# Attention over 128 graphs: a step's chunks start at the fourth slot of the next step, and turned tokens alternate with units of v

## The chip, the core and the metric

One core of a Trainium2 chip. The metric is device microseconds of one execution. TensorE (PE) multiplies and transposes, VectorE (DVE), ScalarE (ACT) and GpSimd (POOL) do the rest, and SyncE (SP) issues nearly all DMAs.

## The reference

128 graphs of 128 nodes with 384 features; 12 heads of 32. For each graph:

```python
h = maximum(layernorm(x), 0)
q, k, v = h @ Wq + bq, h @ Wk + bk, h @ Wv + bv          # split into 12 heads
scores = q @ k.T / sqrt(32) + beta * adj                  # per head, 128 x 128
scores = where(adj > 0, scores, -9e15)
out = softmax(scores) @ v
x = x + out
```

## The kernel before

**Tiling.** A step `s` takes 4 graphs, 512 tokens; there are 32 steps (0 to 31) and a step 32 that only drains. Everything that is multiplied is split into a high and a low part, so that each matrix product is three products (high by high, low by high, high by low). Double buffers are chosen by `par`, the parity of the step.

**Units.** The projection of a step has 13 units (`UNITS`): q0 to q2, k0 to k2 (128 output columns for all 512 tokens, nine matmuls of 512 columns), v0 to v3 (one graph each, nine matmuls of 384 columns) and three "turn" units, which transpose the next step's normalised tokens `hn` for 128 features (four transposes each). A unit fills one of three PSUM banks: `BANK[par][o] = (o + par) % 3`, so unit `o` needs the bank of unit `o - 3`. `bank_free` (L378) makes PE wait until that unit has been taken out: for q and k by the low part on DVE (`low_part`, L598, L604), for a turn by `turn_low` on DVE (L591, L594), for v by ACT's copy (L525).

**Slots.** A step is 12 slots `u`. The matmuls of the units are dealt to the slots by their columns (`PIECES`), and a slot also carries one chunk of attention of the step before: one graph and four heads. In PE's order a slot `u` is: the scores of chunk `u` (L436), the turned probabilities of chunk `u-1` (L444), the slot's pieces of projection (L424) and turns (L404), and the values of chunk `u-2` (L459 to L461). PE takes them strictly in this order. The pieces of the last slots are, before and after the change:

```
slot     before                               after
7        k2 m6-8, v0 m0-4                     the same
8        v0 m5-8, v1 m0-5                     v0 m5-8, turn0, v1 m0-2
9        v1 m6-8, turn0, v2 m0-3              v1 m3-8, turn1, v2 m0
10       v2 m4-8, turn1, turn2                v2 m1-8, turn2
11       v3 m0-8                              the same
```

**DVE's order in a slot** (L653 to L675): `bias_scores` of chunk `u` (mask added, row maximum; L624), where a graph's three chunks are done `invert_sums` (L640), `p_low` of chunk `u-1` (L630), `scale_out` (L645), then the masks (slots 4 and 7; L583, L588), `moments` of the next tokens in slots 0 to 3, and the low parts of units that ended in slot `u-1`. So the low part of k2, which ends in slot 7, is the last thing that DVE does in slot 8. Turns that ended in slot `u-1` follow in slot `u` in the same place.

**ACT's order in a slot**: `p_high` of chunk `u-1` (L535), four exponentials of chunk `u` (L510), the high parts of units that ended in this slot (L517, L525, L530).

**The spread.** q and k come out of the projection stacked by head on partitions. `spread` (L232) copies them, 12 DMAs for q and 12 for k, from `qT`/`kT` to `q_st`/`k_st`, where each head's three parts (high, low, high) lie on 96 partitions. It can start when the low part of q2 or k2 is done, and the first scores of the next step wait for all of it (L431 to L433). All these DMAs, the loads of `xs` and `adjs` and the stores are issued by SP in a written order (L250 to L273), each after its own wait, so that a later one can't pass an earlier one.

**GpSimd** adds the bias of v to x (`add_bias`, L308), normalises the next tokens (`rstd_of`, `normalise`), splits v into high and low (`split_v`, L313) and adds x to the output (`add_x`, L322), in an order written in its `step` (L328 to L355).

The loops: steps 0, 1, 30, 31 and 32 are written out, steps 2 to 29 run in a hardware loop of pairs (L198 to L207).

Of the kernel before, what the change touches and what calls it, by code (L numbers as in the profile page):

```python
# [21 lines left out]
def graph_attention_kernel(nc, x, adj, wq, bq, wk, bk, wv, bv, beta, out):  # L22
# [7 lines left out]
    TOK = G * N  # L30
    SLOTS = G * CH
    SCALE = float(HD) ** -0.5
    VW = HD + 1
# [6 lines left out]
    UNITS = ([("q", c) for c in range(CH)] + [("k", c) for c in range(CH)]  # L40
             + [("v", 0), ("v", 1), ("turn", 0), ("v", 2), ("turn", 1), ("turn", 2), ("v", 3)])
    NB = len(UNITS)
# [36 lines left out]
    with ExitStack() as ctx:  # L79
# [142 lines left out]
        def _(sp):  # L222
# [21 lines left out]
            def store(s, j):  # L244

                wait(sp, added, G * s + j + 1)
                sp.nop(nofuse=True)
                sp.dma_start(out_v[s, j], on[:, j % 2, :]).then_inc(stored[j % 2], 16)

            def step(s, par, looped=False):  # L250
                proj, attend = has(s, looped, 0, STEPS - 1), has(s, looped, 1, STEPS)
                if has(s, looped, 2, STEPS):
                    store(s - 2, G - 1)
                if has(s, looped, 0, STEPS - 3):
                    sp.wait_ge(xb_done, G * (s + 1))
                    sp.wait_ge(normed, G * (s + 1))
                    sp.nop(nofuse=True)
                    sp.dma_start(xs[:, par], x_v[s + 2]).then_inc(x_in[par], 16)
                if proj:
                    spread(s, par, "q")  # L260
                if attend:
                    store(s - 1, 0)
                if has(s, looped, 0, STEPS - 2):
                    sp.wait_ge(mask_done, s + 1)
                    sp.nop(nofuse=True)
                    sp.dma_start(adjs[:], adj_v[s + 1]).then_inc(adj_in, 16)
                if proj:
                    spread(s, par, "k")
                if attend:
                    store(s - 1, 1)  # L270
                    store(s - 1, 2)
                if s is STEPS:
                    store(s - 1, 3)  # L273

# [5 lines left out]
        def _(pool):  # L280
# [47 lines left out]
            def step(s, par, looped=False):  # L328
                proj, attend = has(s, looped, 0, STEPS - 1), has(s, looped, 1, STEPS)
                if proj:  # L330
# [23 lines left out]
                if s is STEPS:  # L354
                    add_x(s - 1, 1 - par, 3)  # L355
# [21 lines left out]
        def _(pe):  # L377
# [49 lines left out]

            def scores(s, par, u):

                j, c, n = u // CH, u % CH, SLOTS * (s - 1) + u  # L430
                if u == 0:  # L431
                    pe.wait_ge(q_in, 16 * 3 * HPC * s)
                    pe.wait_ge(k_in, 16 * 3 * HPC * s)  # L433
                wait(pe, biased_done, HPC * (n - 1))
                for i in range(HPC):
                    mm = pe.matmul(ps_s[u % 2][:, i * N:(i + 1) * N], q_st[0:STACK, 1 - par, i, c, j * N:(j + 1) * N],  # L436
                                   k_st[0:STACK, 1 - par, i, c, j * N:(j + 1) * N], start=True, stop=True)
                mm.then_inc(scores_done, 1)
# [7 lines left out]

            def values_of(g, vp, v, n, odd):

# [5 lines left out]
                for i in range(HPC):  # L454
                    h = c * HPC + i
                    o = ps_o[j % 2][:, h * VW:(h + 1) * VW]
                    high, low = pT[:, odd, 0, i, :], pT[:, odd, 1, i, :]
                    first, second = v1[:, vp, j, h, :], v2[:, vp, j, h, :]
                    pe.matmul(o, high, first, start=True, stop=False)  # L459
                    pe.matmul(o, low, first, start=False, stop=False)  # L460
                    mm = pe.matmul(o[:, 0:HD], high, second, start=False, stop=True)  # L461
                mm.then_inc(pv_done, 1)

            def step(s, par, looped=False):
                proj, attend = has(s, looped, 0, STEPS - 1), has(s, looped, 1, STEPS)
                ahead = has(s, looped, 0, STEPS - 2)
                drain = 2 if not looped and s == STEPS else 0
# [33 lines left out]
        def _(act):  # L501
            act.dma_start(xs[:, 0], x_v[0]).then_inc(x_in[0], 16)

            def exps(s, u):

                n, odd = SLOTS * (s - 1) + u, u % 2
                wait(act, turned, n - 1)
# [30 lines left out]
            def step(s, par, looped=False):  # L538
                proj, attend = has(s, looped, 0, STEPS - 1), has(s, looped, 1, STEPS)
                ahead = has(s, looped, 0, STEPS - 2)  # L540
                drain = 1 if not looped and s == STEPS else 0
                for u in range(SLOTS + drain):
                    n = SLOTS * (s - 1) + u
                    if attend and (looped or n >= 1):
                        p_high(n - 1, (u - 1) % 2)
                    if attend and u < SLOTS:
                        exps(s, u)
                    if proj:
# [18 lines left out]
        def _(dve):  # L567
# [46 lines left out]

            def bias_scores(s, par, u):

                n, odd = SLOTS * (s - 1) + u, u % 2
                dve.wait_ge(scores_done, n + 1)
                wait(dve, exp_done, HPC * (n - 1))
                if u == 0:  # L620
                    dve.wait_ge(mask_done, s)
                dve.nop(nofuse=True)
                for i in range(HPC):
                    dve.tensor_tensor_reduce(out=biased[:, odd, i, :], in0=ps_s[odd][:, i * N:(i + 1) * N],  # L624
                                             in1=mask[:, 1 - par, u // CH, :], scale=-1.0, scalar=3.0e38, op0=ALU.add,
                                             op1=ALU.min, accum_out=neg_max[:, odd, i:i + 1]).then_inc(biased_done, 1)
# [22 lines left out]
            def step(s, par, looped=False):  # L649
                proj, attend = has(s, looped, 0, STEPS - 1), has(s, looped, 1, STEPS)  # L650
                ahead = has(s, looped, 0, STEPS - 2)
                drain = 3 if not looped and s == STEPS else 0
                for u in range(SLOTS + drain):  # L653
                    n = SLOTS * (s - 1) + u
                    ended, late, j = attend and u % CH == 2 and (looped or n > CH), u < CH, (u // CH - 1) % G
                    if attend and u < SLOTS:
                        bias_scores(s, par, u)
                    if ended:
                        invert_sums(s - 1 - late, j)
                    if attend and (looped or n >= 1) and u - 1 < SLOTS:  # L660
                        p_low(n - 1, (u - 1) % 2)
                    if ended:
                        scale_out(s - 1 - late, j)
                    if proj and u == 4:
# [94 lines left out]
```

## Time and profile before

| | |
|---|---|
| median of 3 runs | 1191.81 us (1189.29 to 1191.97) |
| profiled execution | 1193.08 us, span 1191.3 us |
| granted clock of PE, mean | 0.969 |
| busy | PE 1068.0 us (90%), DVE 957.0 (80%), ACT 894.7 (75%), POOL 570.9 (48%) |
| DMA | 138.14 MB, mean 116 GB/s |

The span is from the first to the last instruction; the execution's own time is a little longer. A busy PE is not a PE at its peak, since the ends of its matmuls are modelled. The granted clock is a share of 2.4 GHz. What a step costs is best read from the times at which each slot's scores start (L436, four matmuls): from one to the next is one slot.

### The profile page before, as it was taken

The page shows a single profiled execution, that of the slowest core. Times are in us where ns is not written, and L with a number is a line of the kernel's source. Part 1 is how long each engine was busy: PE and PEld are TensorE (multiplying, and loading weights), DVE is VectorE, ACT ScalarE, POOL GpSimd, SP SyncE. Part 2 cuts the span into 40 slices and gives each one's busy share as a digit, 9 for nine tenths or more (in the row PEclk, how much of TensorE's full clock was granted, in tenths as well). Part 3 has the DMA queues.
Part 4 walks back from the last instruction along what each step waited for, and adds up shares of the span by engine and source line. Part 5 has one row for each costly group of instructions (what it writes and reads, how often), then busy time and mean ns, then how long its engine had stood idle before and what let it go on. Part 6 is the DMA issues. An engine that isn't in the chain of part 4 may idle for free.

```text
span 1191.3 us, 38643 instructions
## 1 busy us (share of the span) xinstructions
PE 1068.0 (90%) x10959; PEld 904.1 (76%) x10959; DVE 957.0 (80%) x4343; ACT 894.7 (75%) x2343; POOL 570.9 (48%) x756
## 2 busy tenths in 40 slices
PE   2799889999999999999999999999999999999875
PEld 1677777877787887778788777778877787888764
DVE  5478778888888888888888888878888888888764
ACT  2377768877787887777788787778877777887764
POOL 3735535445544545454454455454545445454421
PEclk9899999999999999999999999999999999999985
DMA  4434345444444544434554444454444345443330
GB/s 141 112 94 114 110 110 141 122 116 118 115 107 134 142 123 116 119 109 109 136 141 118 114 113 115 115 137 129 118 118 115 105 127 143 129 117 93 80 96 28
DMA packets 91030, 138.14 MB, mean 116 GB/s; under 512 B 15600, under 2 KB 66288, under 8 KB 90864
## 3 DMA queue, kind: packets, MB, share of 16 engines
q1 hardware_dynamic: 90336, 135.85, 42.4%
q14 instruction: 149, 1.22, 0.3%
q10 hardware_dynamic: 528, 0.79, 0.2%
q8 instruction: 17, 0.28, 0.1%
HBM read 35.91 MB, written 25.17 MB: 51 GB/s over the span
## 4 chain that ended last, share of the span: by engine, by line
PE 57%; SPq 14%; DVE 12%; issue 11%; DMA 5%; ACT 1%; POOL 1%; DVEq 1%; POOLq 0%; ACTq 0%
PE ps_p L424 35%; SPq L241 13%; PE ps_t L444 9%; PE ps_s L436 6%; DMA k_st<-kT 4%; DVE biased L624 4%; DVE kT L604 3%; PE ps_o L459 2%; PE ps_o L460 2%; PE ps_o L461 2%; DVE on L645 1%; DVE hT L594 1%; DMA beta_col<-in_L_gnn_beta 1%; PE ps_p L404 1%; ACT probs L510 1%
## 5 line engine op out<-in xcount | busy, mean ns | idle before, releaser
L624 DVE CUSTOM_DVE_ANT_0 biased<-ps_s,mask 128x128 f32<-128x128 f32 x1536 | 351.7, 284 | 181.0 <-PE ps_s L436 166.0
L510 ACT ACTIVATE probs<-biased,neg_max 128x128 f32<-128x128 f32 x1536 | 487.0, 391 | 7.4 <-DVE neg_max L624 7.0
L424 PE MATMUL ps_p<-hT,w 128*128 128x512 f32 x1728 | 475.2, 415 | 3.7 <-DVE w L733 3.7
L535 ACT ACTIVATE pT<-ps_t 128x512 f16<-128x512 f32 x384 | 229.3, 597 | 244.0 <-PE ps_t L444 242.9
L424 PEld LDWEIGHTS ps_p<-hT,w 128*128 128x128 f32 x1728 | 314.1, 193 | 61.5 <-issue 3.9
L630 DVE TENSOR_TENSOR pT<-ps_t,pT 128x512 f16<-128x512 f32 x384 | 256.9, 669 | 17.7 <-ACT pT L535 17.5
L444 PE MATMUL ps_t<-ident,probs 128*128 128x128 f32 x1536 | 241.6, 281 | 16.0 <-ACT probs L510 15.7
L326 POOL TENSOR_TENSOR on<-on,xb 128x384 f32<-128x384 f32 x128 | 128.5, 1004 | 264.4 <-DVE on L645 262.1
L424 PE MATMUL ps_p<-w,hT 128*128 128x384 f32 x1152 | 243.9, 348 | 0.0
L436 PE MATMUL ps_s<-k_st,q_st 96*128 96x128 f16 x1536 | 150.9, 221 | 55.6 <-DMA k_st<-kT 49.4
L424 PEld LDWEIGHTS ps_p<-w,hT 128*128 128x128 f32 x1152 | 193.5, 189 | 2.7
L318 POOL CAST v<-v_f 128x384 f16<-128x384 f32 x128 | 64.7, 505 | 267.4 <-ACT v_f L525 250.0
L459 PEld LDWEIGHTS ps_o<-v,pT 128*128 128x128 f16 x1536 | 123.8, 97 | 81.5 <-issue 53.9
L444 PEld LDWEIGHTS ps_t<-ident,probs 128*128 128x128 f32 x1536 | 166.2, 144 | 21.0 <-ACT probs L510 20.8
L459 PE MATMUL ps_o<-v,pT 128*128 128x33 f16 x1536 | 160.9, 181 | 1.1 <-DVE pT L630 1.1
L460 PE MATMUL ps_o<-v,pT 128*128 128x33 f16 x1536 | 155.7, 178 | 0.0
L461 PE MATMUL ps_o<-v,pT 128*128 128x32 f16 x1536 | 155.7, 177 | 0.0
L436 PEld LDWEIGHTS ps_s<-k_st,q_st 96*128 96x128 f16 x1536 | 90.6, 97 | 59.7 <-issue 59.7
L460 PEld LDWEIGHTS ps_o<-v,pT 128*128 128x128 f16 x1536 | 126.1, 97 | 1.1
L311 POOL TENSOR_TENSOR xb<-xs,bv_row 128x384 f32<-128x384 f32 x128 | 126.5, 1011 | 0.0
L624 DVE DVE_READ_ACCUMULATOR2_ANT neg_max<- 128x1 f32 x1536 | 126.5, 82 | 0.0
L461 PEld LDWEIGHTS ps_o<-v,pT 128*128 128x128 f16 x1536 | 124.2, 96 | 0.0
(59 smaller groups left out, 1073.0 us busy)
## 6 DMA issues: line engine op xcount, KB each, us to landing
q_st<-qT SPq DMA_DIRECT2D x384, 96.0 KB, 2.2
k_st<-kT SPq DMA_DIRECT2D x384, 96.0 KB, 2.1
out<-on SPq DMA_DIRECT2D x128, 192.0 KB, 1.9
xs<-in_x SPq DMA_DIRECT2D x31, 768.0 KB, 4.6
adjs<-in_adj SPq DMA_DIRECT2D x32, 256.0 KB, 2.9
xs<-in_x ACTq DMA_DIRECT2D x1, 768.0 KB, 6.9
k_st<-in_L_gnn_Wq SPq DMA_DIRECT2D x1, 576.0 KB, 5.3
k_st<-in_L_gnn_Wk SPq DMA_DIRECT2D x1, 576.0 KB, 7.4
```

Source lines behind the costliest of these rows:

```text
L241: sp.dma_start(dst[HD * b:HD * (b + 1), par, i], src[HD * i:HD * (i + 1), part]).then_inc(landed, 16)
L326: pool.tensor_tensor(on[:, j % 2, :], on[:, j % 2, :], xb[:, par, j, :], ALU.add).then_inc(added, 1)
L424: mm = pe.matmul(dst, stationary, moving, start=m == 0, stop=m == MMS - 1)
L436: mm = pe.matmul(ps_s[u % 2][:, i * N:(i + 1) * N], q_st[0:STACK, 1 - par, i, c, j * N:(j + 1) * N], k_st[0:STACK, 1 - par, i, c, j * N:(j ...
L444: mm = pe.transpose(ps_t[:, i * N:(i + 1) * N], probs[:, odd, i, :], ident[:])
L459: pe.matmul(o, high, first, start=True, stop=False)
L460: pe.matmul(o, low, first, start=False, stop=False)
L461: mm = pe.matmul(o[:, 0:HD], high, second, start=False, stop=True)
L510: act.activation(probs[:, odd, i, :], biased[:, odd, i, :], ACT.Exp, bias=neg_max[:, odd, i:i + 1], scale=-1.0).then_inc(exp_done, 1)
L535: act.activation(pT[:, odd, 0], ps_t[:].rearrange("p (h q) -> p h q", q=N), ACT.Copy).then_inc(p_high_done, 1)
L624: dve.tensor_tensor_reduce(out=biased[:, odd, i, :], in0=ps_s[odd][:, i * N:(i + 1) * N], in1=mask[:, 1 - par, u // CH, :], scale=-1.0, sc ...
L630: dve.tensor_tensor(pT[:, odd, 1], ps_t[:].rearrange("p (h q) -> p h q", q=N), pT[:, odd, 0], ALU.subtract).then_inc(p_low_done, 1)
```

## The change

Three things (the diff shows, in this order, the constants, `chunk`, SP, GpSimd and PE). A constant `LAG = CH = 3` moves the attention of a step's 12 chunks by three slots: chunk `v` of step `s-1` is scored in slot `v+3` of step `s`, so that the last three are scored in slots 0 to 2 of step `s+1`. In steps 1 to 31 all twelve slots still carry projection; slots 0 to 2 of step 1 have no chunk, and step 32 drains 15 chunks instead of 12. The function `chunk` tells for a slot and a distance behind it which chunk is due, with its step and parity. Second, the units are reordered so that turns alternate with v. Third, SP's and GpSimd's orders are rewritten to fit. Each graph's output is finished three slots later too: graph 0 in slot 8, graph 1 in slot 11, graphs 2 and 3 in slots 2 and 5 of the step after.

```diff
+    LAG = CH
...
     UNITS = ([("q", c) for c in range(CH)] + [("k", c) for c in range(CH)]
-             + [("v", 0), ("v", 1), ("turn", 0), ("v", 2), ("turn", 1), ("turn", 2), ("v", 3)])
+             + [("v", 0), ("turn", 0), ("v", 1), ("turn", 1), ("v", 2), ("turn", 2), ("v", 3)])
...
+        def chunk(s, par, u, behind, looped):
+
+            v = u - LAG - behind
+            back = 2 if v < 0 else 1
+            n = SLOTS * (s - 1) + v
+            if v >= SLOTS or (not looped and not 0 <= n < CHUNKS):
+                return None
+            return n, s - back, par if back == 2 else 1 - par, v % SLOTS
...
                 if has(s, looped, 2, STEPS):
-                    store(s - 2, G - 1)
+                    store(s - 2, 1)
+                    store(s - 2, 2)
+                if proj:
+                    spread(s, par, "q")
+                if has(s, looped, 2, STEPS):
+                    store(s - 2, 3)
                 if has(s, looped, 0, STEPS - 3):
                     sp.wait_ge(xb_done, G * (s + 1))
                     sp.wait_ge(normed, G * (s + 1))
                     sp.nop(nofuse=True)
                     sp.dma_start(xs[:, par], x_v[s + 2]).then_inc(x_in[par], 16)
-                if proj:
-                    spread(s, par, "q")
-                if attend:
-                    store(s - 1, 0)
                 if has(s, looped, 0, STEPS - 2):
                     sp.wait_ge(mask_done, s + 1)
                     sp.nop(nofuse=True)
                     sp.dma_start(adjs[:], adj_v[s + 1]).then_inc(adj_in, 16)
+                if attend:
+                    store(s - 1, 0)
                 if proj:
                     spread(s, par, "k")
-                if attend:
-                    store(s - 1, 1)
-                    store(s - 1, 2)
...
+                if has(s, looped, 1, STEPS):
+                    split_v(s - 1, 1 - par, G - 1)
                 if proj:
                     add_bias(s, par, 0)
                     add_bias(s, par, 1)
-                if has(s, looped, 2, STEPS):
-                    add_x(s - 2, par, G - 1)
+                if older:
+                    add_x(s - 2, par, 2)
                 if proj:
                     add_bias(s, par, 2)
-                    add_bias(s, par, 3)
                 if has(s, looped, 0, STEPS - 2):
                     rstd_of(s + 1)
                     normalise(s + 1, 1 - par)
+                if older:
+                    add_x(s - 2, par, 3)
+                if proj:
+                    add_bias(s, par, 3)
                 if attend:
                     add_x(s - 1, 1 - par, 0)
                 if proj:
                     split_v(s, par, 0)
+                    split_v(s, par, 1)
                 if attend:
                     add_x(s - 1, 1 - par, 1)
                 if proj:
-                    split_v(s, par, 1)
                     split_v(s, par, 2)
-                if attend:
-                    add_x(s - 1, 1 - par, 2)
-                if proj:
-                    split_v(s, par, 3)
...
-                for u in range(SLOTS + drain):
-                    n = SLOTS * (s - 1) + u
-                    if attend and u < SLOTS:
-                        scores(s, par, u)
-                    if attend and u - 1 < SLOTS and (looped or n >= 1):
-                        turn_probs(n - 1, (u - 1) % 2)
+                for u in range(SLOTS + (LAG + 2 if s is STEPS else 0)):
+                    scored, turning, valued = (chunk(s, par, u, behind, looped) for behind in range(3))
+                    if scored:
+                        scores(*scored, (u - LAG) % 2)
+                    if turning:
+                        turn_probs(turning[0], (u - LAG - 1) % 2)
...
-                    if attend and (looped or n >= 2):
-                        late = u < 2
-                        values_of(s - 1 - late, par if late else 1 - par, (u - 2) % SLOTS, n - 2, u % 2)
+                    if valued:
+                        values_of(*valued, (u - LAG) % 2)
```

ACT's and DVE's loops are rewritten in the same way as PE's; within a slot the order of every engine stays as it was.

## Rows read from the trace of the kernel before

**Rows 1.** The profile page, section 4: the chain that ended last, by engine.
```profile
PE 57%; SPq 14%; DVE 12%; issue 11%; DMA 5%; ACT 1%; POOL 1%; DVEq 1%; POOLq 0%; ACTq 0%
```

**Rows 2.** The waits of all engines: waiter <- releaser: us in total, times, longest.
```profile
PE ps_s L436 <- DMA k_st<-kT: 49.4, 29, 5.8
...
PE ps_p L404 <- DVE hT L594: 21.1, 30, 0.7
```

**Rows 3.** Timeline of PE, step 13's slots 8 to 11: start, us, what [idle before].
```profile
504.75 0.38 PE L436 MATMUL ps_s<-k_st,q_st 96*128 96x128 f16 x4
...
505.33 1.98 PE L424 MATMUL ps_p<-w,hT 128*128 128x384 f32 x10
...
507.47 0.38 PE L436 MATMUL ps_s<-k_st,q_st 96*128 96x128 f16 x4
...
508.66 0.60 PE L404 MATMUL ps_p<-ident,hn 128*128 128x128 f32 x4
509.01 0.95 PE L424 MATMUL ps_p<-w,hT 128*128 128x384 f32 x4
...
510.12 0.38 PE L436 MATMUL ps_s<-k_st,q_st 96*128 96x128 f16 x4
...
511.66 0.60 PE L404 MATMUL ps_p<-ident,hn 128*128 128x128 f32 x4
512.96 0.66 PE L404 MATMUL ps_p<-ident,hn 128*128 128x128 f32 x4 [0.70 <-DVE hT L594]
...
513.76 0.38 PE L436 MATMUL ps_s<-k_st,q_st 96*128 96x128 f16 x4
...
518.24 0.40 PE L436 MATMUL ps_s<-k_st,q_st 96*128 96x128 f16 x4 [1.78 <-DMA k_st<-kT]
```

**Rows 4.** Timeline of DVE, low parts, and PE's slot 8 of step 12.
```profile
470.37 0.38 PE L436 MATMUL ps_s<-k_st,q_st 96*128 96x128 f16 x4
...
473.23 0.74 DVE L604 SCALAR_TENSOR_TENSOR kT<-ps_p,bias_qk,kT 128x512 f16<-128x512 f32 x1
...
507.73 0.74 DVE L604 SCALAR_TENSOR_TENSOR kT<-ps_p,bias_qk,kT 128x512 f16<-128x512 f32 x1
...
512.23 0.68 DVE L594 SCALAR_TENSOR_TENSOR hT<-ps_p,hT 128x512 fp32r<-128x512 f32 x1
```

**Rows 5.** Timeline of PE, waits at steps' starts, and seven matmuls of projection.
```profile
522.90 1.89 PE L424 MATMUL ps_p<-hT,w 128*128 128x512 f32 x7
...
588.91 0.40 PE L436 MATMUL ps_s<-k_st,q_st 96*128 96x128 f16 x4 [1.78 <-DMA k_st<-kT]
...
658.33 0.39 PE L436 MATMUL ps_s<-k_st,q_st 96*128 96x128 f16 x4 [1.72 <-DMA k_st<-kT]
...
938.89 0.40 PE L436 MATMUL ps_s<-k_st,q_st 96*128 96x128 f16 x4 [1.68 <-DMA k_st<-kT]
```

**Rows 6.** A stretch by engine: busy us of each, then PE's granted clock, DMA, GB/s.
```profile
519.00:522.00 3.00, 3.00 (x17) 2.04 (x17) 2.18 (x11) 1.76 (x5) 1.89 (x2) 0.53 0.07 23
```

**Rows 7.** Timeline of PE: further first scores, of slots at both ends of the kernel.
```profile
60.95 0.58 PE L436 MATMUL ps_s<-k_st,q_st 96*128 96x128 f16 x4 [5.82 <-DMA k_st<-kT]
...
70.17 0.38 PE L436 MATMUL ps_s<-k_st,q_st 96*128 96x128 f16 x4
...
554.07 0.40 PE L436 MATMUL ps_s<-k_st,q_st 96*128 96x128 f16 x4 [1.31 <-DMA k_st<-kT]
...
623.54 0.39 PE L436 MATMUL ps_s<-k_st,q_st 96*128 96x128 f16 x4 [1.30 <-DMA k_st<-kT]
...
1148.63 0.38 PE L436 MATMUL ps_s<-k_st,q_st 96*128 96x128 f16 x4 [2.39 <-issue]
...
1176.31 0.59 PE L436 MATMUL ps_s<-k_st,q_st 96*128 96x128 f16 x4
...
1179.27 0.59 PE L436 MATMUL ps_s<-k_st,q_st 96*128 96x128 f16 x4
```

**Rows 8.** Timeline of SP's queue: the twelve copies of one spread of k.
```profile
544.71 7.51 SPq L241 DMA_DIRECT2D k_st<-kT  x12
```

More of the change, by code:

```diff
@@ L31, in graph_attention_kernel @@
     SLOTS = G * CH
+    CHUNKS = STEPS * SLOTS
+    LAG = CH
     SCALE = float(HD) ** -0.5
@@ L266, in step @@
                     sp.dma_start(adjs[:], adj_v[s + 1]).then_inc(adj_in, 16)
+                if attend:
+                    store(s - 1, 0)
                 if proj:
                     spread(s, par, "k")
-                if attend:
-                    store(s - 1, 1)
-                    store(s - 1, 2)
                 if s is STEPS:
-                    store(s - 1, 3)
+                    for j in range(1, G):
+                        store(s - 1, j)
             run_steps(sp, step)
@@ L329, in step @@
                 proj, attend = has(s, looped, 0, STEPS - 1), has(s, looped, 1, STEPS)
+                older = has(s, looped, 2, STEPS)
+                if has(s, looped, 1, STEPS):
+                    split_v(s - 1, 1 - par, G - 1)
                 if proj:
@@ L347, in step @@
                 if proj:
-                    split_v(s, par, 1)
                     split_v(s, par, 2)
-                if attend:
+                if s is STEPS:
                     add_x(s - 1, 1 - par, 2)
-                if proj:
-                    split_v(s, par, 3)
-                if s is STEPS:
                     add_x(s - 1, 1 - par, 3)
@@ L426, in project, with scores @@
                     mm.then_inc(proj_done, 1)
[L428 to L433, printed above, removed]
+            def scores(n, g, gp, v, odd):
+                j, c = v // CH, v % CH
+                if v == 0:
+                    pe.wait_ge(q_in, 16 * 3 * HPC * (g + 1))
+                    pe.wait_ge(k_in, 16 * 3 * HPC * (g + 1))
                 wait(pe, biased_done, HPC * (n - 1))
                 for i in range(HPC):
-                    mm = pe.matmul(ps_s[u % 2][:, i * N:(i + 1) * N], q_st[0:STACK, 1 - par, i, c, j * N:(j + 1) * N],
-                                   k_st[0:STACK, 1 - par, i, c, j * N:(j + 1) * N], start=True, stop=True)
+                    mm = pe.matmul(ps_s[odd][:, i * N:(i + 1) * N], q_st[0:STACK, gp, i, c, j * N:(j + 1) * N],
+                                   k_st[0:STACK, gp, i, c, j * N:(j + 1) * N], start=True, stop=True)
                 mm.then_inc(scores_done, 1)
@@ L445, in turn_probs, with values_of @@
                 mm.then_inc(turned, 1)
-            def values_of(g, vp, v, n, odd):
+            def values_of(n, g, gp, v, odd):
                 j, c = v // CH, v % CH
@@ L457, in values_of @@
                     high, low = pT[:, odd, 0, i, :], pT[:, odd, 1, i, :]
-                    first, second = v1[:, vp, j, h, :], v2[:, vp, j, h, :]
+                    first, second = v1[:, gp, j, h, :], v2[:, gp, j, h, :]
                     pe.matmul(o, high, first, start=True, stop=False)
@@ L464, in step @@
             def step(s, par, looped=False):
-                proj, attend = has(s, looped, 0, STEPS - 1), has(s, looped, 1, STEPS)
-                ahead = has(s, looped, 0, STEPS - 2)
-                drain = 2 if not looped and s == STEPS else 0
-                for u in range(SLOTS + drain):
-                    n = SLOTS * (s - 1) + u
-                    if attend and u < SLOTS:
-                        scores(s, par, u)
-                    if attend and u - 1 < SLOTS and (looped or n >= 1):
-                        turn_probs(n - 1, (u - 1) % 2)
+                proj, ahead = has(s, looped, 0, STEPS - 1), has(s, looped, 0, STEPS - 2)
+                for u in range(SLOTS + (LAG + 2 if s is STEPS else 0)):
[4 more added lines that the diff above has]
+                        turn_probs(turning[0], (u - LAG - 1) % 2)
                     if proj:
@@ L502, in _, with exps @@
             act.dma_start(xs[:, 0], x_v[0]).then_inc(x_in[0], 16)
-            def exps(s, u):
-                n, odd = SLOTS * (s - 1) + u, u % 2
+            def exps(n, odd):
                 wait(act, turned, n - 1)
@@ L538, in step @@
             def step(s, par, looped=False):
[L539 to L547, printed above, removed]
+                proj, ahead = has(s, looped, 0, STEPS - 1), has(s, looped, 0, STEPS - 2)
+                for u in range(SLOTS + (LAG + 1 if s is STEPS else 0)):
+                    scored, turning = (chunk(s, par, u, behind, looped) for behind in range(2))
+                    if turning:
+                        p_high(turning[0], (u - LAG - 1) % 2)
+                    if scored:
+                        exps(scored[0], (u - LAG) % 2)
                     if proj:
@@ L613, in low_parts, with bias_scores @@
                         turn_low(s + 1, 1 - par, ps_p[BANK[par][o]], UNITS[o][1])
-            def bias_scores(s, par, u):
-                n, odd = SLOTS * (s - 1) + u, u % 2
+            def bias_scores(n, g, gp, v, odd):
                 dve.wait_ge(scores_done, n + 1)
                 wait(dve, exp_done, HPC * (n - 1))
-                if u == 0:
-                    dve.wait_ge(mask_done, s)
+                if v == 0:
+                    dve.wait_ge(mask_done, g + 1)
                 dve.nop(nofuse=True)
@@ L649, in step @@
             def step(s, par, looped=False):
[L650 to L657, printed above, removed]
+                proj, ahead = has(s, looped, 0, STEPS - 1), has(s, looped, 0, STEPS - 2)
+                for u in range(SLOTS + (LAG + 3 if s is STEPS else 0)):
+                    scored, turning, _, valued = (chunk(s, par, u, behind, looped) for behind in range(4))
+                    ended = valued is not None and valued[3] % CH == CH - 1
+                    if scored:
+                        bias_scores(*scored, (u - LAG) % 2)
                     if ended:
-                        invert_sums(s - 1 - late, j)
-                    if attend and (looped or n >= 1) and u - 1 < SLOTS:
-                        p_low(n - 1, (u - 1) % 2)
+                        invert_sums(valued[1], valued[3] // CH)
+                    if turning:
+                        p_low(turning[0], (u - LAG - 1) % 2)
                     if ended:
-                        scale_out(s - 1 - late, j)
+                        scale_out(valued[1], valued[3] // CH)
                     if proj and u == 4:
```

2 lines of the change are left out of this document (1 added, 1 removed).

## The prediction

> **What bounds the kernel now.** I read three views in this order. The chain that ended last is mostly PE's, with SP's queue second [rows 1]: PE is the bound, and something that SP issues interrupts it. The waits say what: PE's first scores of a step wait for the copies of k, 49.4 us in 29 waits, and a turn waits for a low part on DVE, 21.1 us in 30 [rows 2]. Then PE's timeline by slots, from one slot's scores to the next. The last four slots of step 13 begin at 504.75, 507.47, 510.12 and 513.76, and the next step at 518.24 [rows 3], so they take 2.72, 2.65, 3.64 and 4.48 us. The third holds the wait for DVE, the fourth the wait for k. The wait of 0.70 us in the third is shown from the modelled end of the transposes before; they could follow at a pitch of 0.35 us (508.66 to 509.01), so 511.66 + 0.35 = 512.01 was possible and 0.95 us were lost. After the values of a slot the modelled end hides about 0.13 us in the same way, so a boundary wait of 1.78 costs 1.91.
>
> Two steps in which the clock stays up show the pace: from 554.07 over 588.91 to 623.54, 69.47 us [rows 5, 7]. Their boundary waits are 1.78 and 1.30 us (3.34 lost with the two 0.13), their waits for DVE 2 x 0.95. The rest, 64.23 us, is 32.1 us of work a step. As it is, a step takes 34.7 us where the clock holds.
>
> **What the change takes away.** In slot 3 of the next step the copies of k are long there. The low part of k2 ends at 508.47, the twelve issues take 7.51 us [rows 4, 8] and the last lands some 2.2 us later, so k is ready within 10 us, and there are 18 us from slot 8 to slot 3 of the next step. The written order of SP puts `store(s-1, 0)` ahead of this spread; DVE's scaling and GpSimd's addition for it end about 4.0 us into slot 8, a few tenths after the low part of k2. The load of `xs` (now behind the spread of q and `add_bias(3)`) goes out in slot 8, more than three slots ahead of its reader. Nothing here is on the path: the cover is some 4 to 7 us of slack, and if it were gone, the boundary wait would merely come back in part, 1.9 us at most by today's size. So −1.91 and −1.43 us in turn, 1.67 a step. The rows of GpSimd are not needed on the path either: `normalise` ends about two slots before turn0 asks for it.
>
> The reordering takes away today's DVE wait in slot 10: turn2 needs unit 8's bank, which held turn0 and now holds v1, copied by ACT a slot earlier. −0.95 us.
>
> **What it adds: three bank waits.** The order of units decides who needs whose bank, `o` that of `o - 3`.
>
> (a) v1 is now unit 8 and starts in slot 8. It needs the bank of k2, whose low part is DVE's last work in slot 8. Before, unit 8 was turn0 in slot 9, at 508.66, and the low part of k2 had ended at 508.47: it just fitted [rows 3, 4]. Now v1 would be ready 0.58 us (scores, turned probabilities) + 4 x 0.18 (rest of v0) + 0.42 (turn0 with its switch) = 1.72 us into the slot, at 1.72 + 504.75 = 506.47. It may start at 508.47 + 0.05 = 508.52, 3.77 into the slot. That is 2.05 us lost. In step 12 the low part ends at 473.97, 3.60 after 470.37, and 1.93 are lost; the two parities alternate so in all steps of the loop. Mean 1.99. DVE's own order and load in slots 2 to 8 don't change (the same operations; it is busy without a gap from slot 2 to 5), so I expect no other time for k2. Behind v1 in PE's order stand the values of this slot and the scores of the next: all wait. Bounds: nothing, if DVE reached k2 two microseconds sooner, and 2.05 + 0.95 (today's DVE wait) = 3.0 if DVE fell further behind.
>
> (b) v2's first matmul is in slot 9 and needs turn0's bank, freed by DVE. Today the like low part ends at 512.91 and lets PE go at 512.96, 2.84 after the scores of its slot at 510.12 [rows 3, 4]. v2 would be ready at 0.58 + 6 x 0.18 + 0.42 = 2.09: 0.75 lost (0.50 shown as idle). Bounds 0 and 0.95.
>
> (c) q0 after a step of even parity needs turn2's bank, freed some 3.27 into slot 11, and is ready at 3.12: 0.15 in every second step, 0.08 a step. Bounds 0 and 0.3.
>
> Sum for a step whose clock holds: 32.1 + 1.99 + 0.75 + 0.08 = 34.92, against 34.7. The wait has not gone, it has moved from the boundary to slot 8.
>
> **The clock.** PE's granted clock falls to its lower level (1.2 of 2.4 GHz) after some of the boundary waits. After the one of 1.78 us at 518.24 it was 0.53 on average from 519 to 522 [rows 6], and that step took 554.07 − 518.24 = 35.83 us against 34.63 for the one from 588.91 to 623.54, with the same closing wait and no fall [rows 3, 5, 7]: a fall costs 1.2. The wait of 1.72 us at 658.33 brought one too, that of 1.78 at 588.91 did not, and the largest of the smaller ones, 1.68 at 938.89, did not [rows 5]. The new wait (a) would be shown as 2.05 − 0.25 = 1.80 us in odd steps, above all of these, and 1.68 in even ones, at the edge (0.25 is what the modelled end of transposes hides). Two of three fell at 1.72 to 1.78, so for 1.80 I take three of four: 11 of the 15 odd steps, and none of the even ones. A fall here costs a little less than 1.2, because the slower slot 9 uses up part of wait (b): I take 1.0, and 11 us in all.
>
> The Trainium skill bears on this (TensorE: Matmul & The Clock Gate, section "A second HAM failure mode: psum-queue depth-cycling"): micro-idles between groups of matmuls that cycle through PSUM banks made the clock swing between its two levels. By it all 30 steps would fall, since each now has two bank waits; the rows here show both outcomes for waits of this size and none of two waits so close together, so it is the third rival.
>
> **The ends.** Start: step 1's first scores wait 5.82 us for k until 60.95, and slot 3 begins at 70.17 [rows 7]. Now slots 0 to 2 of step 1 project meanwhile, from 55.1 on, 22 matmuls of some 0.24 us (seven take 1.89 with the drain [rows 5]), and slot 3 begins when k is there, at 61.0. Then 30 steps of 34.92 = 1047.6, to 1108.6. Then slots 3 to 11 of step 31, which has no turns: 34.92 − 8.1 for three slots − 3 x 0.45 for the turns − 0.75 for wait (b) + 0.3 for a longer wait (a) − 0.1 for (c) = 24.9, to 1133.5. The drain has 15 chunks instead of 12. Its slots take 1179.27 − 1176.31 = 2.96 us; 14 of them, two at the full clock of some 2.65, are 40.8, to 1174.3 for the last scores. What follows them took 1191.3 − 1179.27 = 12.0. Span 1186.3, and 1.8 around it: 1188.1, with 11 for the clock 1199.1 against 1193.08 of the same execution, so +6.0. The median of the runs lies 1.3 below that execution: 1197.8, say 1198.
>
> **The rivals.** *The clock holds* (the other side). If the waits of 1.68 and 1.80 us don't bring it down, the sum ends at 1188.1 − 1.3 = 1187: faster. What decides is a single wait's size, with the edge between 1.68 and 1.78. For it: the largest wait that left the clock alone was 1.78, nearly as long. Against it: 1.72 was enough once. *A few falls*, 2 to 8: 1189 to 1195; for it speaks that today few boundaries bring a fall, the mean granted clock being 0.969 with the slow start and drain in it. *Every step falls*: 30 x 1.0 = 30, 1217. For it speaks that wait (b) follows three microseconds after (a), so there is more idle close together than today. *No bank wait in slot 8*, because DVE is early enough or v1's piece is held by something else anyway: 34.92 − 1.99 a step, 1187 − 60 = 1127. Against it: k2's low part ended at the same distance from its slot's start, 3.59 to 3.74 us, in every step from 1 to 30 (two of them in [rows 4]). *The new orders of SP or GpSimd bring a wait of their own*, up to the size of today's boundary wait: 1.7 x 30 = 51, 1249. The slack above speaks against it.
>
> **Chances.** Forecast 0.43; clock holds 0.22; a few falls 0.20; every step 0.08; no wait 0.05; new orders 0.02. A measurement of this kernel can tell about 0.3%, 3.6 us, from no change, so the same is 1188.2 to 1195.4. Faster: clock holds and no wait, 0.27. Same: a few falls, and a little of the forecast's lower end, 0.21. Slower: the rest, 0.52. The range goes from the clock that holds, 1186, to 24 falls, 1211; the forecast's own, 8 to 16 falls, is 1195 to 1204.
>
> **What would show it.** In the profile after, PE's first scores no longer wait for DMA. Instead L424 (v1) waits for DVE L604, 1.7 to 1.8 us in each of some 30 steps, about 52 us in all, and again for DVE L594, 0.5 us. Slot 8 takes 4.6 us and slot 9 3.4; slots 0 to 7 are unchanged, slot 10 is 2.84 and slot 11 2.57. Slot 3 of step 1 begins near 61. In steps with a fall the granted clock is low at the end of slot 8 and in slot 9. It is wrong if PE's idle time in slot 8 is under 1 us, or if steps without a fall are shorter than 34.5 us or longer than 35.3.

## The result and the profile after

The changed kernel takes 1261.57 us (median of 4 runs, 1260.21 to 1261.98) against 1191.89 for the kernel before: ratio 1.0586, 95% interval 1.0568 to 1.0603. It is slower by 5.9%, 64 us above the forecast.

The waits of the changed kernel (waiter <- releaser: us in total, times, longest), where L440 is the projection, L452 the scores, L460 the turned probabilities, L522 the exponentials, L633 the mask and maxima:

```profile
DVE biased L633 <- PE ps_s L452: 185.9, 176, 4.7
...
PE ps_t L460 <- ACT probs L522: 61.3, 28, 3.5
...
PE ps_p L440 <- DVE kT L614: 57.5, 31, 2.1
DVE biased L633 <- issue: 55.7, 13, 4.4
ACT probs L522 <- DVE neg_max L633: 54.9, 14, 5.1
...
PE ps_p L440 <- DVE hT L604: 14.3, 27, 0.5
...
PE ps_s L452 <- DMA k_st<-kT: 3.8, 1, 3.8
```

Two lines were forecast: the wait of the scores for k has gone (49.4 us in 29 waits before [rows 2], one wait now), and the projection waits for the low part of k2 in 31 steps, 57.5 us, where I had said about 52: 1.68 to 1.70 us in 16 steps, 2.02 to 2.05 in the 14 even steps from 2 to 28, and 2.12 in step 31. Three lines in a row were not: 13 times DVE stands for "issue", that is for nothing that the profile shows, 4.3 us each; ACT's exponentials wait for DVE, and PE for the exponentials.

PE's timeline from slot 8 of step 5 to slot 3 of step 6 of the changed kernel (start, us, what, [idle before <- releaser]):

```profile
223.86 0.38 PE L452 MATMUL ps_s<-k_st,q_st 96*128 96x128 f16 x4
...
227.51 0.80 PE L440 MATMUL ps_p<-w,hT 128*128 128x384 f32 x3 [1.69 <-DVE kT L614]
228.47 0.38 PE L452 MATMUL ps_s<-k_st,q_st 96*128 96x128 f16 x4
...
231.31 0.44 PE L440 MATMUL ps_p<-w,hT 128*128 128x384 f32 x1 [0.53 <-DVE hT L604]
231.91 0.38 PE L452 MATMUL ps_s<-k_st,q_st 96*128 96x128 f16 x4
...
234.71 0.38 PE L452 MATMUL ps_s<-k_st,q_st 96*128 96x128 f16 x4
...
237.26 0.38 PE L452 MATMUL ps_s<-k_st,q_st 96*128 96x128 f16 x4
...
240.21 0.38 PE L452 MATMUL ps_s<-k_st,q_st 96*128 96x128 f16 x4
244.00 1.10 PE L460 MATMUL ps_t<-ident,probs 128*128 128x128 f32 x4 [3.41 <-ACT probs L522]
244.74 3.03 PE L440 MATMUL ps_p<-hT,w 128*128 128x512 f32 x7
247.93 0.38 PE L452 MATMUL ps_s<-k_st,q_st 96*128 96x128 f16 x4
```

Slot 8 takes 228.47 − 223.86 = 4.61 us (forecast 4.6), slot 9 3.44 (3.4), slot 10 2.80 (2.84), slot 11 2.55 (2.57). Compare the same slots of before, 2.72, 2.65, 3.64, 4.48 [rows 3]. Then the surprise: slot 1 of step 6, from 240.21 to 247.93, takes 7.72 us instead of 2.61. PE stands 3.41 us before its turned probabilities, and after that the granted clock is 0.59 on average from 244 to 248 us: the seven matmuls take 3.03 us instead of 1.89 [rows 5]. DVE says why. Its timeline at that place, in the changed kernel:

```profile
237.33 0.68 DVE L604 SCALAR_TENSOR_TENSOR hT<-ps_p,hT 128x512 fp32r<-128x512 f32 x1
242.31 0.29 DVE L633 CUSTOM_DVE_ANT_0 biased<-ps_s,mask 128x128 f32<-128x128 f32 x1 [4.30 <-issue]
```

The scores for this work began at 237.26 and took 0.38 us, and DVE was free at 238.01; it takes them at 242.31. This happens in 13 places, between steps 3 and 4, 5 and 6, up to 27 and 28. Those are the 13 jumps back of the loop over pairs of steps (steps 2 to 29). Between the two steps of a pair there is nothing like it. The kernel before has the same loop, and at a jump of its own DVE shows:

```profile
587.05 1.28 DVE L594 SCALAR_TENSOR_TENSOR hT<-ps_p,hT 128x512 fp32r<-128x512 f32 x2
590.20 0.29 DVE L624 CUSTOM_DVE_ANT_0 biased<-ps_s,mask 128x128 f32<-128x128 f32 x1 [1.87 <-PE ps_s L436]
```

Here the profile blames PE, because PE's scores at 588.91 waited for k themselves [rows 5]. But those scores were done half a microsecond later, and DVE came only at 590.20. The line "issue" had a hint of it before the change too, in the full list of waits: `DVE biased L624 <- issue: 11.7, 6, 2.1`. I had not followed it.

So a step that ends in a jump takes 40.0 us and the others 35.1, counted from slot 3 to slot 3, against my 34.92 for all. The 35.1 still hold the longer wait for k2 of the even steps: slot 8 is 4.95 us there and 4.61 in the odd ones. DVE takes the scores of slot 7 some 1.0 us after their start in the even steps and 0.6 in the odd ones.

### The profile page after: what moved, and what is told of

Its sections match the earlier page's. It is cut to its first block, busy times and chain, and to the rows that moved or that the text cites. A ratio compares the mean times of both kernels' runs of the same rounds, so it can differ in the third digit from the quotient of the medians.

```text
span 1260.2 us, 38643 instructions
## 1 busy us (share of the span) xinstructions
PE 1092.1 (87%) x10959; PEld 921.1 (73%) x10959; DVE 958.7 (76%) x4343; ACT 895.3 (71%) x2343; POOL 572.2 (45%) x756
## 4 chain that ended last, share of the span: by engine, by line
PE 63%; DVE 19%; issue 13%; SPq 1%; DVEq 1%; DMA 1%; POOL 1%; ACT 1%; POOLq 0%; ACTq 0%
PE ps_p L440 38%; PE ps_t L460 10%; DVE biased L633 7%; PE ps_s L452 6%; DVE kT L614 3%; PE ps_o L475 3%; PE ps_o L476 2%; PE ps_o L477 2%; DVE hT L604 2%; DVE on L654 2%; DVE pT L639 1%; PE ps_p L420 1%; SPq L253 1%; DVE mask L598 1%; DVE neg_max L633 1%
## 5 line engine op out<-in xcount | busy, mean ns | idle before, releaser
L633 DVE CUSTOM_DVE_ANT_0 biased<-ps_s,mask 128x128 f32<-128x128 f32 x1536 | 351.7, 285 | 243.4 <-PE ps_s L452 185.9
L522 ACT ACTIVATE probs<-biased,neg_max 128x128 f32<-128x128 f32 x1536 | 487.1, 391 | 55.9 <-DVE neg_max L633 54.9
L440 PE MATMUL ps_p<-hT,w 128*128 128x512 f32 x1728 | 480.2, 418 | 4.1 <-DVE w L740 3.3
L440 PEld LDWEIGHTS ps_p<-hT,w 128*128 128x128 f32 x1728 | 319.5, 197 | 67.3 <-DVE hT L604 4.3
L440 PE MATMUL ps_p<-w,hT 128*128 128x384 f32 x1152 | 257.5, 355 | 71.8 <-DVE kT L614 57.5
L460 PE MATMUL ps_t<-ident,probs 128*128 128x128 f32 x1536 | 247.6, 286 | 61.3 <-ACT probs L522 61.3
L440 PEld LDWEIGHTS ps_p<-w,hT 128*128 128x128 f32 x1152 | 197.6, 192 | 88.4 <-DVE kT L614 65.0
L460 PEld LDWEIGHTS ps_t<-ident,probs 128*128 128x128 f32 x1536 | 170.0, 147 | 67.2 <-ACT probs L522 67.1
L452 PE MATMUL ps_s<-k_st,q_st 96*128 96x128 f16 x1536 | 150.5, 221 | 3.8 <-DMA k_st<-kT 3.8
L633 DVE DVE_READ_ACCUMULATOR2_ANT neg_max<- 128x1 f32 x1536 | 126.7, 82 | 0.0
L333 POOL TENSOR_TENSOR v<-v_f,v 128x384 f16<-128x384 f32 x128 | 113.7, 889 | 10.3
```

The costliest lines, as they stand in the source:

```text
L440: mm = pe.matmul(dst, stationary, moving, start=m == 0, stop=m == MMS - 1)
L452: mm = pe.matmul(ps_s[odd][:, i * N:(i + 1) * N], q_st[0:STACK, gp, i, c, j * N:(j + 1) * N], k_st[0:STACK, gp, i, c, j * N:(j + 1) * N], ...
L460: mm = pe.transpose(ps_t[:, i * N:(i + 1) * N], probs[:, odd, i, :], ident[:])
L522: act.activation(probs[:, odd, i, :], biased[:, odd, i, :], ACT.Exp, bias=neg_max[:, odd, i:i + 1], scale=-1.0).then_inc(exp_done, 1)
```

## The experiments

The place of DVE's loop is counted in instructions of DVE's program: it starts at 192 in the changed kernel and at 226 in the kernel before, and is 417 long in both.

**Where DVE's loop lies.** `e1` and `e2` put waits that are long satisfied at the head of DVE's program: 34 of them in the changed kernel (`e1`, the loop now starts at 226), 222 in the kernel before (`e2`, at 448, which is 256 beyond 192). No other engine's code changes.

```diff
+            for _ in range(34):
+                dve.wait_ge(x_in[0], 16)
+                dve.nop(nofuse=True)
             dve.wait_ge(small_in, 16 * 4)
```

> The changed kernel with 34 waits that are long satisfied put at the start of DVE's program, so that DVE's loop lies at the place in its code where it lay before the change (instruction 226 instead of 192); nothing else moves. Theory A (DVE reloads its code after the loop's jump back, and how long it stands depends on where the loop lies): the stand of 4.3 us after each of 13 jumps falls to the 1.9 us of before, steps of 40.0 us become some 37.6, and the time falls by 31 us to about 1230. Theory B (the stand belongs to the new order or to what collides with it): nothing changes, 1261.

> The kernel before with 222 satisfied waits at the start of DVE's program, which puts DVE's loop at the place of the changed kernel's, modulo 256 instructions. Theory A: DVE now stands some 4.3 us after its last work of a loop's second step instead of 1.9, about 1.5 to 2.4 us of it uncovered by the wait for k, 13 times: 1212 to 1223, with up to 8 us once for the waits themselves. Theory B: 1192 to 1200.

Measured: 1213.62 us (ratio to before 1.0194, 1.0161 to 1.0227), 48 us less than the changed kernel, and 1246.21 (1.0459, 1.0425 to 1.0493), 55 more than the kernel before. 8.6 us of these 55 are the waits themselves (step 1's scores begin at 69.54 instead of 60.95 [rows 7]). Both go the way of theory A; both are larger than I had put them. DVE at the jump, in e1:

```profile
233.43 0.68 DVE L604 SCALAR_TENSOR_TENSOR hT<-ps_p,hT 128x512 fp32r<-128x512 f32 x1
235.98 0.29 DVE L633 CUSTOM_DVE_ANT_0 biased<-ps_s,mask 128x128 f32<-128x128 f32 x1 [1.87 <-issue]
```

1.87 us here and 1.8 to 2.1 over the 13 jumps; in the kernel before DVE is idle there for 1.9 to 2.1 us at twelve jumps, part of them under PE's name, and for 2.8 at the first. The same order of work stands for 4.3 or 1.9 us according to where its code lies; moving the old order to the other place brings the long stand there (3.8 to 4.5 us at each jump of e2).

The packets that the queue of instructions brings say the same. The pages of the changed kernel and, below it, of e1 have:

```profile
q14 instruction: 97, 0.79, 0.2%
q14 instruction: 84, 0.69, 0.2%
```

That is 13 packets of some 8 KB more, one for each jump. At the jump shown above the changed kernel gets two while DVE stands (the view of the queues counts one from 237.5 to 239 us and one from 240 to 242.3), and DVE goes on at 242.31. In e1 there is one, from 233.5 to 235.9, and DVE goes on at 235.98. The profile doesn't say for which engine a packet is; but between these two kernels only DVE's program differs.

**No jump at all.** `e5` is the changed kernel and `e7` the kernel before, with steps 2 to 29 written out.

```diff
-            with eng.Fori(1, STEPS // 2 - 1) as pair:
-                step(2 * pair, 0, True)
-                step(2 * pair + 1, 1, True)
+            for pair in range(1, STEPS // 2 - 1):
+                step(2 * pair, 0)
+                step(2 * pair + 1, 1)
```

> The changed kernel with steps 2 to 29 written out instead of looped: no jump back on any engine, everything else in the same order. Theory A (all that exceeds my forecast is the reload after the jump): the 13 steps of 40.0 us become 34.9 like the others, 13 x 5.1 = 66 us less, 1195, near my forecast of 1198. Theory B (something in the new order stalls DVE once in two steps, whatever the code): 1261.

> The kernel before written out without a loop. Theory A says that its reloads were covered by the wait for k at the step's start, all but 0.6 us of DVE's stand: 0.2 to 0.6 us in 13 steps, so 3 to 8 us less, 1183 to 1188. If the jump cost the kernel before as much as it costs the changed one, 1125.

Measured: e5 1195.44 us, ratio 1.0029 (1.0012 to 1.0046), 66.1 less than with the loop. DVE's waits for issue after a jump are gone, and most steps are 34.7 to 34.9 us, or some 0.7 to 0.8 more with a fall of the clock. e7 gives 1203.70 (1.0087, 1.0064 to 1.0111): slower than with its loop, not faster. Its boundary waits have grown and vary. The waits of e7:

```profile
PE ps_s L436 <- issue: 57.4, 31, 3.5
...
PE ps_s L436 <- DMA k_st<-kT: 6.2, 1, 6.2
```

63.6 us together. Before they were 55.6: 49.4 for k [rows 2] and, in the steps that were written out already, `PE ps_s L436 <- issue: 6.2, 3, 2.6`. SP's twelve copies of k take longer in some steps, as in this one of e7, against 7.51 [rows 8]:

```profile
439.64 8.75 SPq L241 DMA_DIRECT2D k_st<-kT  x12
```

The waits are 8 us longer and the clock falls more often (11 times between start and drain against 6, each some 1.2 us); less the reload that is gone (some 4 us, see below) that is 10 of the 12 us. Why SP pauses is to be seen in the instruction queues: q8 brings 88 packets of 16 KB in e7 and 17 in the kernel before, and in e7 each of the 21 spreads of k that take over 7.6 us has one of them in it, none of the 11 others has. So SP seems to wait for code of its own; no run takes this apart. What the kernel before paid for DVE's reload e7 can't show beside this, only that it was not the 66 us of the other order. Its own trace can: slot 1 after a jump takes 2.95 us on average against 2.61 elsewhere, some 4 us in 13 jumps.

**The order of units and the later attention apart.** `e3` is the changed kernel with the old order of units, `e4` the kernel before with the new one.

```diff
-             + [("v", 0), ("turn", 0), ("v", 1), ("turn", 1), ("v", 2), ("turn", 2), ("v", 3)])
+             + [("v", 0), ("v", 1), ("turn", 0), ("v", 2), ("turn", 1), ("turn", 2), ("v", 3)])
```

> The changed kernel with the units in the order of before (turn0 in slot 9, both turn1 and turn2 in slot 10). If the bank waits in slots 8 and 9 cost what I worked out (1.99 + 0.75 + 0.08 us a step) and the old wait in slot 10 comes back (0.95), each step is 1.87 us shorter, 30 steps 56 us: 1205, with the stand of DVE after the jump as before. If v1's wait only hides another one behind it, 1240 to 1261.

> The kernel before with only the order of units changed. The bank waits (2.0 in slot 8, 0.75 in slot 9) come before the wait for k at the step's start, whose copies go on meanwhile, so they use it up: the step then takes what PE's own path gives, about 34.9 us, and the time is 1190 to 1200. If bank waits and the wait for k add up, 1248.

Measured: e3 1212.60 (1.0180, 1.0148 to 1.0212), e4 1215.06 (1.0206, 1.0172 to 1.0240). In e3 a step without a jump takes 33.36 us instead of 35.07 and the stand remains (3.6 to 4.1 us; slot 1 after a jump is 6.7 to 7.9 us). In e4 a step without a jump takes 34.83: the bank waits do use up the wait for k, as expected. A step after a jump takes some 36.6 where the clock holds, with 13 waits of DVE for issue of 2.0 us each: with the wait for k DVE's reload lost its cover. Each half of the change alone uncovers the reload.

**The later attention with the old order of units, without the stand.** `e6` is e3 written out, `e8` is e3 with the 34 waits of e1.

> The later attention with the old order of units, written out without a loop: steps of 33.4 us throughout instead of 33.4 and 38.6 in turn, 13 x 5.3 = 69 us less than with the loop: 1144, faster than the kernel before by 4%. If the reload is not the cause, 1212.

> The later attention with the old order of units and the loop, with DVE's loop moved by 34 instructions as in the first experiment. There the slot after the jump fell from 7.6 to 3.8 us. The same here: 7.0 to some 3.8, 13 x 3.3 = 43 us less than 1212.6: 1170, faster than the kernel before by 1.8%.

Measured: e6 1141.59 us (0.9578, 0.9562 to 0.9594), e8 1159.55 (0.9728, 0.9705 to 0.9751). Both beat the kernel before; the later attention was a gain that two other things buried. (Eleven of e8's jumps stand 1.5 to 1.8 us, the first 2.1 and the last 3.55, for which the trace gives no reason.)

**The bank wait in slot 8.** `e11` is e5 with one low part moved on DVE; `e16` is the same with the loop kept and 64 satisfied waits ahead.

```diff
+                    if proj and u == 8:
+                        low_parts(s, par, 7, ahead)
                     if scored:
                         bias_scores(*scored, (u - LAG) % 2)
...
-                    if proj and u >= 1:
+                    if proj and u >= 1 and u != 8:
                         low_parts(s, par, u - 1, ahead)
```

> The changed kernel without the loop, and DVE takes the low part of k2 at the start of slot 8, ahead of the mask and maxima of that slot's chunk, instead of at its end. If the wait in slot 8 is for this one instruction, it goes (v1's bank is free 1.7 us into the slot): slot 8 is 2.7 us instead of 4.6, the chunk's exponentials end some 0.2 to 0.4 us late for slot 9, and the clock has no wait above 1.7 us left to fall after. 30 x 1.7 and some 8 us for the clock less than 1195.4: 1136 to 1144. If v1 would have waited there anyway, 1190 to 1197.

> The changed kernel with its loop kept, DVE's loop at a place with the short stand (moved by 64) and the low part of k2 first in slot 8. If the two causes are separate, they add: 1211 less the 56 us that the low part's place brought without the loop, 1155, faster than the kernel before by 3%. If they cover each other, more than 1165.

Measured: e11 1139.87 us (0.9553, 0.9516 to 0.9589), e16 1155.71 (0.9701, 0.9675 to 0.9728). PE around slot 8 of step 6 in e11:

```profile
244.29 0.39 PE L452 MATMUL ps_s<-k_st,q_st 96*128 96x128 f16 x4
245.65 0.60 PE L420 MATMUL ps_p<-ident,hn 128*128 128x128 f32 x4
246.93 0.38 PE L452 MATMUL ps_s<-k_st,q_st 96*128 96x128 f16 x4
247.58 0.63 PE L460 MATMUL ps_t<-ident,probs 128*128 128x128 f32 x4 [0.26 <-ACT probs L522]
```

Slot 8 is 2.64 us instead of 4.61 and has no wait; slot 9 grows from 3.44 to 3.89 us, with 0.26 shown as the wait for the late exponentials, as expected. A step takes 33.2 to 33.4 instead of 34.7 to 34.9, and no step shows a fall of the clock. The wait was for that one instruction. e16 came within 1 us of its sum, so the two causes add up.

**Another order of units.** `e12`, without the loop:

```diff
-             + [("v", 0), ("turn", 0), ("v", 1), ("turn", 1), ("v", 2), ("turn", 2), ("v", 3)])
+             + [("v", 0), ("v", 1), ("v", 2), ("turn", 0), ("v", 3), ("turn", 1), ("turn", 2)])
```

> The later attention without the loop, units in the order v0, v1, v2, turn0, v3, turn1, turn2: k2's bank is asked for by v2 in slot 9, just after it is free, the banks of turns by turn2 alone, a slot later, and q0's bank held v3 or turn1. One wait of 0.75 us in slot 11 instead of 0.95 in slot 10 and 0.6 in every second slot 0: steps of 33.0 us instead of 33.4, 1131. If the three units that end in slot 11 make DVE late for slot 0, 1141 to 1150.

Measured: 1148.37 (0.9634, 0.9600 to 0.9667), 17 above what I expected. Steps are 33.6 us, slot 11 takes 4.10:

```profile
255.84 0.66 PE L420 MATMUL ps_p<-ident,hn 128*128 128x128 f32 x4 [1.33 <-DVE hT L604]
```

turn2 waits longer for turn0's low part than where it stood before, since in slot 11 DVE also scales a graph's output ahead of it. I had left that out.

**What of the place sets the stand.** One run each of the changed kernel, with 16, 64, 100 and 128 satisfied waits ahead of DVE's work (`e14`, `e9`, `e15`, `e10`), and with 34 inside the loop (`e13`), whose edit is:

```diff
+                    if looped and par == 1 and u == 9:
+                        for _ in range(34):
+                            dve.wait_ge(x_in[0], 16)
+                            dve.nop(nofuse=True)
                     if ended:
```

> DVE's loop moved by 16 instructions (192 to 208). 0 and 128 stand long, 34 and 64 short; nothing tells where between 0 and 34 the level changes. Short: 1213; long: 1262. A value between them would speak against two levels.

> The changed kernel, DVE's loop moved by 64 instructions (its start at 256 instead of 192; 226 stood shorter). If the stand grows or shrinks steadily with the place, it is now 0 to 1 us and the slot after the jump some 2.9 us; if it has only two levels, it is 2.1 or 4.3 us, 1214 or 1262.

> DVE's loop moved by 100 instructions (start 292). With pieces of 128 instructions the level must change back between 64 and 128. Short: 1213; long: 1262.

> The changed kernel, DVE's loop moved by 128 instructions (start at 320). If code comes in pieces of 128 instructions, this place is like the changed kernel's own: a stand of 4.3 us, 1262. If the pieces are larger, it may be the short one, 1214.

> The changed kernel with 34 satisfied waits inside DVE's loop (slot 9 of its second step), so that the loop starts where it did (192) and ends at 643 instead of 609, the place where the kernel before ends it. If the length of the stand is set by where the jump leaves (something still under way there), it is the short one, some 2.1 us: 1214, and up to 1.5 us in 14 steps for the waits themselves. If it is set by where the jump lands, it stays 4.3: 1262 to 1280.

| loop starts at | DVE's stand at a jump, us | slot 1 after a jump, us | time, us |
|---|---|---|---|
| 192 (changed kernel) | 4.2 to 4.4 | 7.5 to 7.7 | 1261.57 |
| 208 (e14) | 1.8 to 2.1, the first 2.4 | 3.7 to 4.3 | 1212.30 |
| 226 (e1) | 1.8 to 2.1 | 3.7 to 4.0 | 1213.62 |
| 256 (e9) | 1.8 to 2.0 | 3.7 to 3.9 | 1211.44 |
| 292 (e15) | 2.6 to 2.8, mostly under PE's name | 4.5 to 4.7, the first 5.7 | 1217.96 |
| 320 (e10) | 4.2 to 4.5 | 7.5 to 7.9 | 1263.64 |
| 448 (e2, the kernel before) | 3.8 to 4.5 | not comparable | 1246.21 |
| 192, ends 34 later (e13) | 4.3 to 4.4 | 7.1 to 8.2 | 1319.33 |

The jump in e13:

```profile
249.86 0.29 DVE L633 CUSTOM_DVE_ANT_0 biased<-ps_s,mask 128x128 f32<-128x128 f32 x1 [4.29 <-issue]
```

It is where the jump lands, not where it leaves: e13 keeps 4.3. (Its waits cost far more than I had allowed: DVE passes over them in 2.2 us, and slots 9 and 10 of that step take 9.8 us together instead of 6.2, so of e13 only the stand is read.) 128 instructions further on, the place is as bad as the first, and 256 further on too (e2); between them it is short, except at 292. There the stand is neither of the two values that I had expected, so there are not just two levels. The packets of q14 follow: 84 in e14, e1 and e9, 97 in the changed kernel, e13 and e15, 98 in e10. In e15 the second one comes sooner than in the changed kernel, some half a microsecond after the first. A small delay goes with the place too: DVE takes the scores of slot 7 of even steps 1.0 us after their start with the loop at 192 and at 320, and 0.6 with it at 256 (e9); that is the longer wait for k2 in every second step. All this fits code that comes in pieces of 128 instructions: land at the end of one, and two have to come, one after the other, before the first slots' work can go; land further from its end, and one is enough, or the second comes sooner. That the border between pieces lies just behind 192 is read from the stands alone, and so is the size.

## Why the prediction was wrong

- **The boundary wait as pure loss.** The part "What the change takes away" booked 1.67 us a step as gained and named what could be late next: the copies, SP, GpSimd. It didn't ask what else used that wait. DVE reloads its code after the loop's jump, 1.9 us in the kernel before, and the wait for k lay over nearly all of it. This is the step that failed: the sum has no term for what comes to light after a jump. e1, e2 and e5 show it: of the 69.7 us by which the changed kernel is slower, 66 go when the 13 jumps go. In the other steps the 1.67 us were gained as booked.
- **"DVE's own order and load … don't change".** True of the work, and not enough: the change made the steps ahead of DVE's loop 34 instructions shorter, so the loop lands at another place, where a reload takes 4.3 us. That is 48 of the 66 us (e1), the fall of the clock behind each long stand and the longer wait for k2 included. The other 18 are the short reload, uncovered (e1 against e5, 1213.62 to 1195.44).
- **The bank waits.** Right in place, releaser and size. (a) is shown as 1.68 to 1.70 us in steps 1 to 30 of e5 (1.87 in step 20), and costs 1.96 (slot 8 is 4.61 us there and 2.65 in e11), where I had 1.99; in the changed kernel it is shown as 2.02 to 2.05 in every second step. (b) is shown as 0.53. In steps without a jump and without a fall e5 has 34.73 and 34.91 where the sum says 34.92. e11 takes (a) away by its cause. The rival *no bank wait in slot 8* is out.
- **The clock.** 9 of the first 30 steps of e5 show a slow slot 9 (4.1 to 4.2 us instead of 3.44), where I had 11, and a fall costs 0.7 to 0.8 us, where I took 1.0. So neither *the clock holds* nor *every step falls*. That 9 lies near 11 is luck. The two parities of (a), on which the 11 rested, were not there: the wait is 1.68 to 1.70 us with a fall and without, in steps of both parities, and after the one of 1.87 slot 9 was as fast as ever. So the size of this wait alone doesn't decide; what does stays open. My edge was also read from too few rows: in the kernel before a wait of 1.74 us at 798.57 brought a fall too, three of four then, and the largest of the smaller ones was 1.69, at 379.37. What the Trainium skill says of small idles between groups that cycle through PSUM banks (TensorE: Matmul & The Clock Gate, section "A second HAM failure mode: psum-queue depth-cycling") is borne out in so far as the clock does swing with two bank waits a step; that every step would fall, as I had read it, is not.
- **The ends.** Slot 3 of step 1 begins at 63.2, not 61.0, 2 us late. SP's new order puts the load of `xs` (issued at 50.61) right ahead of this spread (from 51.83), and the twelve copies of k take 4.7 us each to land (median) where they took 2.2 before; the remaining wait for k in the changed kernel is that one, 3.8 us.
- **The sum without the loop's jumps** was 1198, and e5 gives 1195.4. That is the part that held, with terms that cancel: the steps were 0.1 us shorter and the falls some 4 us cheaper in all, and the start came 2 us later.
- **SP's and GpSimd's new orders** bring no wait in the steps: PE waits for k once, at the start (those 2 us), and never for GpSimd once the steps run. e5 has the same orders.

The Trainium skill states the rule that I missed (Runtime: NRT & Kernel Launch, section "Instruction fetch mechanics"): a taken branch whose target isn't in the part of the code that the engine holds makes it fetch that part by DMA before it can go on. The traces agree, with 1.8 to 2.1 us (e1) or 4.2 to 4.4 (the changed kernel) on DVE at each of 13 jumps and one or two packets of instructions meanwhile.

## What to carry to other kernels

Before removing a wait that all engines share, look at every engine across it: what an engine does there in the wait's shadow becomes visible when the shadow goes, and a loop's jump back is such a thing. A stand with the releaser "issue" that comes once per iteration is the sign; where another engine is late at the same point, it can stand under that engine's name. When code ahead of a loop grows or shrinks, the loop lands elsewhere; compare with the loop written out, or with satisfied waits ahead of it, before judging the change. And when units share PSUM banks in rotation, a new order is judged by who frees the bank that each unit gets, and where in that engine's slot this is done.

## What the runs showed of the hardware

A DVE that jumps back over 417 instructions stood for 1.8 to 2.1 us at nearly all jumps where the loop starts at 208, 226 or 256, for 2.6 to 2.8 at 292 and for 3.8 to 4.5 at 192, 320 and 448, which fits a period of 128 instructions. The long stand goes with one more packet of 8 KB on the instruction queue at each jump (97 against 84). Writing the loop out is not free either: in e7 SP's twelve copies took up to 8.95 us instead of 7.51, each time with a 16 KB packet of instructions among them. 34 satisfied waits in a row inside DVE's loop took 2.2 us of DVE and cost PE 3.6 us (e13); 222 at the start of its program delayed step 1 by 8.6 us (e2). With two bank waits in each step, of 1.69 and 0.53 us, the granted clock fell to its lower level in 9 of 30 steps of e5; without the first of them it fell in none (e11).
